# Filler matmuls taken out of a pipelined kernel, its first keys computed earlier, and three softmax sums moved from GpSimd to TensorE

## The reference

```
xn = layernorm(x)
# layer 0: causal attention, 16 heads of 8, keys and values from a 32-wide latent; beside it 8 experts, top 2 of them
lat = layernorm(xn @ W_dkv); k = rope(lat @ W_uk); v = lat @ W_uv; q = rope(xn @ W_q)
x = x + (softmax(causal(q k^T)) v) @ W_o + sum_e gate_e * (relu(xn @ W1[e] + b1[e]) @ W2[e] + b2[e])
xn = layernorm(x)
# layer 1: attention of 16 heads, mixed with two attentions of 4 heads of 32; beside it a gated three-layer FFN
ctx = softmax(mod * q k^T) v
ctx = 0.3 * ctx + 0.7 * mha4(xn)          # "ca"
ctx = 0.85 * ctx + 0.15 * mha4(ctx)       # "mc"
x = x + ctx @ W_o + ffn(xn)
```

## Time and profile before

| what | value |
|---|---|
| runs, median (lowest to highest) | 1742.61 us (1740.61 to 1746.71) |
| the profiled execution: time, span | 1751.61 us, 1749.9 us |
| mean granted TensorE clock in it | 0.949 of 2.4 GHz |
| busy share PE, DVE, ACT, POOL | 88%, 69%, 60%, 47% |
| POOL's sums for the denominators (L1423) | 64 instructions, 149.2 us busy |

### The profile page before, as it was taken

One profiled execution on the slowest core, in us unless ns is written; L12 is line 12 of the kernel. 1 busy time (PEld: TensorE's weight loads), 2 busy tenths in 40 slices (PEclk: granted clock), 3 DMA queues, 4 the chain that ended last, 5 costly groups with the idle time before them and its releaser, 6 DMA issues.

```text
span 1749.9 us, 33947 instructions
## 1 busy us (share of the span) xinstructions
PE 1539.8 (88%) x11449; PEld 655.0 (37%) x11449; DVE 1202.1 (69%) x3135; ACT 1055.2 (60%) x2322; POOL 817.4 (47%) x728
## 2 busy tenths in 40 slices
PE   2587799889999999999999999999899999889877
PEld 1353353235333543345333543345333533232222
DVE  6553578667885789667975788678976677477523
ACT  2273375667657766676656765677557765736542
POOL 4246355435644555454645455354654461513142
PEclk9998698999999999999999999999999999979877
DMA  5851471136211541236212631145203620201010
GB/s 210 259 152 50 128 195 33 46 93 181 79 42 61 154 118 55 67 93 180 63 34 75 166 103 48 63 117 157 69 29 96 185 80 7 61 13 37 0 37 6
DMA packets 138876, 159.35 MB, mean 91 GB/s; under 512 B 15744, under 2 KB 100304, under 8 KB 137808
## 3 DMA queue, kind: packets, MB, share of 16 engines
q1 hardware_dynamic: 134608, 148.79, 29.1%
q0 software_dynamic: 4096, 8.40, 1.6%
HBM read 115.96 MB, written 40.85 MB: 90 GB/s over the span
## 4 chain that ended last, share of the span: by engine, by line
PE 61%; DVE 11%; ACT 10%; issue 8%; POOL 6%; DMA 3%; SPq 2%; POOLq 0%; ACTq 0%; DVEq 0%
PE banks L450 58%; DVE negmax L862 6%; ACT probs L1202 3%; ACT hm L1271 3%; POOL psums L1423 2%; DMA qkc<-relm 1%; ACT L1202 1%; DVE h L1086 1%; PE banks L714 1%; POOL halves L1379 1%; PE banks L667 1%; SPq L1554 1%; POOL w L1442 1%; ACT h L1320 1%; DVE h L1081 0%
## 5 line engine op out<-in xcount | busy, mean ns | idle before, releaser
L1202 ACT ACTIVATE probs<-banks 128x512 f32<-128x512 f32 (+3 forms) x1216 | 582.5, 534 | 362.1 <-PE banks L450 340.2
L862 DVE TENSOR_REDUCE negmax<-banks 128x1 f16<-128x512 f32 x768 | 491.9, 685 | 157.5 <-PE banks L450 153.9
L858 DVE CUSTOM_DVE_ANT_0 scr<-banks,mask_row 128x384 bf16<-128x384 f32 (+3 forms) x512 | 230.2, 487 | 156.0 <-PE banks L450 146.0
L450 PE MATMUL banks<-kp,qs 32*128 32x512 f16 (+3 forms) x1024 | 239.6, 360 | 64.4 <-DMA kp<-relk 21.1
L450 PE MATMUL banks<-probs,vp 128*32 128x512 f32 (+3 forms) x2048 | 241.1, 544 | 0.2 <-POOL probs L1375 0.2
L450 PE MATMUL banks<-qs,kp 32*128 32x512 f16 (+3 forms) x1024 | 218.3, 352 | 23.3 <-ACT probs L1202 15.9
L1463 POOL TENSOR_TENSOR h_lo<-h,h_hi 128x512 f16<-128x512 f32 x96 | 114.5, 1211 | 211.8 <-ACT h_hi L1314 116.0
L1403 POOL TENSOR_TENSOR hl<-hm,hh 128x512 f16<-128x512 f32 x120 | 139.9, 1168 | 136.3 <-DVE hh L1028 136.3
L1423 POOL TENSOR_TENSOR psums<-psums,probs 128x1024 f32<-128x1024 f32 x64 | 149.2, 2356 | 113.1 <-PE banks L450 113.1
L1271 ACT ACTIVATE hm<-banks,wt 128x128 f32<-128x128 f32 x480 | 137.7, 374 | 72.2 <-PE banks L450 71.7
L450 PE MATMUL banks<-qkc 97*128 97x512 f16 (+1 forms) x512 | 169.6, 404 | 8.8 <-DVE negmax L862 3.0
(11 more groups left out here) (211 smaller groups left out, 2457.1 us busy)
## 6 DMA issues: line engine op xcount, KB each, us to landing
wt<-wexp SPq DMA_DIRECT2D x120, 258.0 KB, 3.0
wt<-wexp SPq DMA_DIRECT2D x120, 256.0 KB, 3.0
qkc<-relm SPq DMA_DIRECT2D x96, 128.0 KB, 3.2
qs<-relq SPq DMA_DIRECT2D x64, 128.0 KB, 2.5
kp<-relk SPq DMA_DIRECT2D x64, 128.0 KB, 2.6
relm<-halves SPq DMA_DIRECT2D x32, 256.0 KB, 2.1
xg<-xslots SPq DMA_DIRECT2D x24, 256.0 KB, 3.0
yslots<-yv SPq DMA_DIRECT2D x24, 256.0 KB, 3.5
```

The lines of the kernel that those rows point to most:

```text
L450: return nc.tensor.matmul(psum[rows_, bank, cols_], lhsT, rhs, start=start, stop=stop)
L858: v.tensor_tensor_reduce(scr[:, s, 0:kw], psum[:, SCO + s, 0:kw], mask_row[:, T - kw:T], -1.0, 3e38, ALU.add, ALU.min, negmax[:, g.n % 2, ...
L862: v.tensor_reduce(negmax[:, g.n % 2, NC * h + c:NC * h + c + 1], psum[:, SCO + s, 0:kw], AX.X, ALU.max, negate=True).then_inc(sem("max"), 1)
L1202: a.activation(keys(g, c)[:, 2 * pair + s, q0:T], psum[:, TRA + s, q0:T], ACT.Exp, scale=SCALE[main(g)]).then_inc(sem("exp"), 1)
```

## The change

Three edits. The fillers of `turn_over` go, in every period. The first batch's keys get a stage of their own, 8 steps earlier, which puts them ahead of `pos`, `gates` and `starts` of its routing, and the first two stores of the weights move from G = -11 and -10 to -4 and -3, behind the first two `spread`s; one lot of `keep_warm` of the first batch moves from G = 52 to 47. For the last three 4-head groups (`direct`) PE sums every block of keys itself, POOL's sums go, and POOL multiplies quarter by quarter.

```
-TURNS = (6, 3, 3)
-MOVE = {"route": {0: 6}, "warm0": {-1: -6}, "warm1": {-1: 6}, "front": {}, "prep": {0: 11},
+MOVE = {"route": {0: 6}, "warm0": {-1: -6}, "warm1": {-1: 6}, "front": {}, "keys": {0: -8}, "prep": {0: 11},
-AT.update({("w_store", i): at for i, at in enumerate((-11, -10, -4, 2), 0)})
-AT.update({("turn", i): at for i, at in enumerate((72, 6, 47), 0)})
+AT.update({("w_store", i): at for i, at in enumerate((-4, -3, -2, 2), 0)})
...
+    elif head.split("_")[0] in ("k0", "k0r"):
+        STAGE[name_] = "keys"
...
+        def direct(g):
+            return g.mix >= len(MIXES) - 3
...  value(), PE
-                    last.then_inc(sem("pv"), 1)
-                    if not main(g) and c == NC - 1:
+                    if direct(g):
+                        if c == 0:
+                            own("n", "den", g.n)
+                        if c == NC - 1:
+                            last.then_inc(sem("pv"), 1)
+                        for h in range(GH):
+                            last = mm(N, slice(0, T), ones[:, :], keys(g, c)[:, h, :], c == 0, c == NC - 1,
+                                      rows_=slice(32 * h, 32 * h + 32))
+                        last.then_inc(sem("n_full" if c == NC - 1 else "pv"), 1)
+                    else:
+                        last.then_inc(sem("pv"), 1)
+                    if not main(g) and not direct(g) and c == NC - 1:
...  the loop of PE
-                    turn_over(G)
...  mixing(), DVE
                                 if k == NC - 1:
                                     ins.then_inc(sem("n_taken"), 1)
+                                elif direct(g):
+                                    ins.then_inc(sem("quarter"), 1)
...  exp_unit(), ACT: no wait for psums
+                                if not direct(before):
+                                    act.wait_ge(sem("psums"), 4 * before.mix + 2 * k - 1 + pair)
...  mixing(), POOL
+                            pool.wait_ge(sem("out_taken"), g.n + 1)
+                            if direct(g):
+                                for k in range(NC - 1):
+                                    pool.wait_ge(sem("quarter"), (NC - 1) * (g.mix + 3 - len(MIXES)) + k + 1)
+                                    p_.tensor_tensor(out=oc[:, ch(k)], in0=oc[:, ch(k)], in1=r_b[:, ch(k)], op=ALU.mult)
+                            left = slice(P * (NC - 1), T) if direct(g) else slice(0, T)
                             taken(pool, "n", "den", g.n)
-                            pool.wait_ge(sem("out_taken"), g.n + 1)
-                            p_.tensor_tensor(out=oc[:, :], in0=oc[:, :], in1=r_b[:, :], op=ALU.mult).then_inc(sem("oc"), 1)
+                            p_.tensor_tensor(out=oc[:, left], in0=oc[:, left], in1=r_b[:, left], op=ALU.mult).then_inc(sem("oc"), 1)
...  the loop of POOL
-                        if not main(g) and 2 <= j < 6:
+                        if not main(g) and not direct(g) and 2 <= j < 6:
```

More of the change, by code:

```diff
@@ L146 @@
 AT.update({("y_store", i): at for i, at in enumerate((20, 29, 37, 43), 0)})
-AT.update({("w_store", i): at for i, at in enumerate((-11, -10, -4, 2), 0)})
-AT.update({("turn", i): at for i, at in enumerate((72, 6, 47), 0)})
-AT.update({("warm0", i): at for i, at in enumerate((34, 37, 43, 47, 48, 51, 58, 65, 66, 70), 0)})
+AT.update({("w_store", i): at for i, at in enumerate((-4, -3, -2, 2), 0)})
+AT.update({("warm0", i): at for i, at in enumerate((34, 37, 43, 47, 48, 51, 53, 65, 66, 70), 0)})
 AT.update({("warm1", i): at for i, at in enumerate((178, 181, 186, 188, 192, 192, 194, 194, 197, 199), 0)})
@@ L594, in opening @@
                             project(N, W(w), xT[:, :]).then_inc(sem("n_full"), 1)
[L596 to L603, removed]
                 def keep_warm(G):
@@ L1196, in exp_unit @@
                             if k in (1, 2):
-                                act.wait_ge(sem("psums"), 4 * before.mix + 2 * k - 1 + pair)
+                                if not direct(before):
+                                    act.wait_ge(sem("psums"), 4 * before.mix + 2 * k - 1 + pair)
                             elif pair == 0:
```

## The result

| | median (lowest to highest) | profiled execution: time, span, mean clock |
|---|---|---|
| before | 1744.11 us (1740.61 to 1746.71, 4 runs) | 1751.61, 1749.9 us, 0.949 |
| after | 1762.34 us (1761.01 to 1765.82, 4 runs) | 1763.57, 1761.4 us, 0.932 |

The ratio is 1.0097, 95% interval [1.0071, 1.0123]: slower by 18 us, where 1745 was forecast and the range ended at 1758.

The account below looks back on a forecast made before the run. The prediction took PE as the bound, with 61% of the chain that ended last. From 1742.6 us it took 9 (start), 0.9 (warm lot) and 1.2 (tail) and added 13.4 (falls): 1744.9, forecast 1745, range 1729 to 1758.

Parts of the forecast that it names:

- Direct gain 0: At the fillers' three places: removing 87 matmuls gains 0 us, since PE still waits for ACT or DVE; bounds 0 to 37.
- first three: First lot of three fillers per period: eight gaps of 2.1 us, 0.5 of them falling at 0.9 us each, 3.6 us lost.
- The falls' cost, 13.4 us: Where fillers stood: 22 longer PE gaps bring falls of the granted clock to 1.2 GHz, 13.4 us lost; bounds 0 to 35.
- the start: First batch: earlier keys and later stores bring the first weight load from 67.22 to about 58, gain 9 us; bounds 4 to 12.
- warm lot: First batch: four matmuls moved ahead of its last sums leave the chain there, gain 0.9 us; bounds 0 to 1.7.
- the tail: Last three 4-head groups: PE's own sums gain 1.2 us net; bounds 3.5 gain to 2.5 loss.
- six: Lot of six fillers per period: seven gaps of 2.3 us, 0.8 of them falling at 1.5 us each, 8.4 us lost.
- second three: Second lot of three fillers per period: seven gaps of 1.7 us, 0.4 of them falling at 0.5 us each, 1.4 us lost.
- the last group's 1.8: Last 4-head group: 1 us from no wait for POOL's sums and 0.8 from POOL's smaller last product, gain 1.8 us.
- the group of `ca` of batch 7: Third direct group, which waits for no sum: eight more matmuls on PE cost 1.8 us where PE bounds, 1.5 taken.
- The rival of the many falls: Falls at nearly every bare place at full price, 16 at 1.57 us, 25 us lost: 1757 us; chance 0.2.
- The clock's rival: Without fillers the clock holds, or nearly, with about 2 more falls (3 us): 1734 us; chance 0.28.

Follow-up runs that it names:

- e5: The changed kernel with all fillers back and PE's direct sums only for the last two 4-head groups, early keys kept: 1735.68 us, ratio 0.9934 to before.
- e2: The kernel before with only the 87 fillers and their waits taken out: 1768.04 us, ratio 1.0126 to before.
- e12: The changed kernel as it is, run again on another chip: 1762.8 us, ratio 1.0111 to before.
- e1: The changed kernel with the fillers put back where they were, the keys' and direct sums' edits kept: 1741.61 us, ratio 0.9971 to before.
- e9: e5 with the three lots of fillers taken out: 1758.52 us, ratio 1.0074 to before.
- e3: The kernel before with only the early keys, the two later stores and the earlier warm lot, fillers kept: 1740.49 us, ratio 0.997 to before.
- e4: The kernel before with only the direct sums by PE in the last three 4-head groups, fillers kept: 1747.93 us, ratio 1.0007 to before.
- e6: The changed kernel with the lots of six fillers back, both lots of three still out: 1751.26 us, ratio 1.0027 to before.
- e11: e5 with a fourth lot of three fillers at G = 58 of each period: 1738.29 us, ratio 0.9973 to before.
- e10: e5 with fillers of 128 columns instead of 512, same number, places and waits: 1742.49 us, ratio 0.9994 to before.
- e8: The changed kernel with the fillers back in doubled lots (12, 6, 6): 1750.82 us, ratio 1.0021 to before.
- e7: The changed kernel with the fillers' waits back but not one matmul: 1757.14 us, ratio 1.0051 to before.

## Why the prediction was wrong, point by point

**Direct gain 0: right.** Stretches that keep their clock take the same time with and without fillers: 38.68 us in after and in e5. (From G = 16 to 40 the four kernels without fillers are 2.5 us shorter in all, on average, the only trace of a gain.) The gaps were read a little too high in number: of the eight places of the first three, five have the gap of 2.2 us; at G = 86 and 166 PE has shorter ones.

**The falls' cost, 13.4 us: this is the step that failed.** Measured 22 us (e2) and 24 us (e12 over e1, e9 over e5). The mechanism and its sign were as put; the number and places were not. The result is 16 us slower than the forecast (18.2 over before, where 2.3 was the sum): 9 of them are this term, 5 the start with its warm lot, 2 the tail. To split it, I took the stretches of a period apart and compared the mean of four kernels without fillers (after, e2, e9, e12) with that of five with them (before, e1, e3, e4, e5), summed over the middle:

| stretch | lot in it | us at 1.2 GHz, with / without | forecast us | measured us |
|---|---|---|---|---|
| G = 72 to 80 | six | 3.4 to 6.8 / 20.5 to 27.3 | 8.4 | 3.2 |
| G = 0 to 16 | first three | 26.8 to 31.7 / 55.7 to 57.7 | 3.6 | 8.1 |
| G = 40 to 56 | second three | 17.1 to 30.7 / 23.9 to 44.4 | 1.4 | 5.2 |
| the others | none | 6.8 to 15.6 / 6.8 to 13.7 | 0 | -1.6 |
| all of the middle | | 58.8 to 77.7 / 115.7 to 134.4 | 13.4 | 14.9 |

The places of the falls are what ties them to the lots. At G = 72 and 73 all 24 stretches of the four kernels without fillers have one, and none of the 30 with; at the first three, from G = 240 on, it is 19 of 20 against 0 of 25. (Of the us at 1.2 GHz in the second row, 23 to 34 are of the first of its seven stretches, in every kernel.)

In the middle alone the sum of 13.4 is nearly met, but by luck: three errors cancel. At the six the number was right (a fall at each), the price was not: the six stretches of after take 22.47 to 23.08 us, 0.5 to 1.1 more than a whole one of 21.97, and not 1.5. I put this down to ACT's exponentials, which hold PE for part of it; no run shows this by itself. With the lots, seven of the thirty stretches fall later, at G = 75 behind the wait for `w`, and take 23.55, so that 3.2 us are left. At the first three I took half of the lots at 0.9 us; it was five of six in after and all in e9 and e12 (one of the six, at G = 166, falls with fillers too), at 1.2 (39.96 and 39.85 against 38.68). At the second three, 0.4 of the lots at 0.5 us; there a fall costs 1.5 (39.8 against 38.3), and falls came at G = 40 to 45 too, where no lot had stood.

The rest came outside these 550 steps. In the pairs that differ in the fillers alone, e1 and e12, e5 and e9, the spans differ by 19.5 and 23.7 us, of which the middle has 15.6 and 18.7, what lies behind step 632 has 4.9 and 5.3, and the start -0.9 and -0.3. Most of the tail's loss, 3.5 us, comes between the first maxima of steps 688 and 692, where no lot stood. There e9 and e12 stand at 1.2 GHz for 13.7 us, e1 and e5 for 3.4. But e6, which has the only lot behind step 632, stands so for 13.7 us too, and so do before and e11 with all their fillers, while e2 without them has 6.8 us (262.2 and 258.4 us behind step 632). So the forecast had nothing for the tail, two pairs out of three show a loss there, and its cause stays open. And the medians stand above what profiled executions show, which for e2 and e12 were the lowest of their runs; a term that varies from execution to execution can't be sized from one execution.

**The start, -9: right in its steps, too large in its worth.** Step 80 came 9.0 us earlier in the two traces compared; in the three traces with the old start it stands at 182.0 to 185.0 us, in the eleven with the new one at 175.1 to 178.6, which is 7 us on average, and the timed gain of e3 is 5 (1 to 9). **The warm lot** wasn't separated from it. **The tail, -1.2:** the last group's 1.8 is 1.2 (from the first maximum of step 732 to the end 44.6 us in after and e12, 45.8 in before and e3), the group of `ca` of batch 7 cost 2.5 instead of 1.5; all three, e4, +0.07%.

**The rival of the many falls** (16 at 1.57 us, 25 us, 1757) comes nearest to what came, though not by its sum: the traces show 13 more falls on average, at 1.1 us each in the middle. It was given 0.2. What argued against it, that ACT and DVE hold PE behind 15 of the 22 gaps, was true for the six's place, where it was not applied, and false for the first three, where it was. With its 25 us, the start's 5 instead of 9, no gain from the warm lot and the tail, and 1744 for before it gives 1764. The range ended at 1758, below that: this rival was its slow case, and it had every other term at its likeliest value.

**The clock's rival** (1734) did not come. One argument for it was misread: the two windows of rows 3 have the same busy time, 8.51 and 8.50 us, but 48 and 56 matmuls, so the one that fell had done less work. The Trainium skill (TensorE: Matmul & The Clock Gate, "HAM oscillation — how this bites in real kernels") puts the drops down to idle gaps longer than any here; this trace disagrees, with a fall behind nearly every gap of 2.2 to 2.3 us (the one at 1154.20 above is the exception). Its next section, "A second HAM failure mode: psum-queue depth-cycling", tells of a kernel whose clock swung because of frequent short pauses; e10's stretch with pauses of 0.60 and 1.17 us agrees with that one.

## What to carry to other kernels

Matmuls that nobody reads can be worth keeping where they stand wholly behind a wait: 87 of them cost nothing and were worth 22 to 24 us of 1745; by the waits alone, which divide one of the gaps, some 10 us of this were kept. Before taking them out, look at the windows just behind each and count how many periods keep clock 1.00 with them; a lot protects its own stretch alone, and doubled it runs out of cover. Price a fall by the stretch that it would land in (0.5 to 1.1 us at the six's place, 1.2 to 1.6 at the others), once for every period, and measure the tail apart.

## What was not expected

- With all fillers kept the clock fell seldom but not never: 7 to 15 falls in the middle (4 in e11), most at G = 40 to 45 and 55 to 60 behind PE waits of 1.06 and 0.68 us or none. No kernel had none.
- A granted clock of 1.00 in the first 70 us may stand for no record at all. The same window of e12, then of e1:

```profile
39.00:61.00 22.00, 8.03 (x32) 3.62 (x31) 11.51 (x33) 3.61 (x6) 7.49 (x7) 0.50 0.78 248
```

```profile
39.00:61.00 22.00, 9.08 (x35) 3.96 (x35) 11.36 (x33) 3.61 (x6) 7.83 (x7) 1.00 0.79 253
```

But the matmuls take as long in both. The eight transposes of `xg` in e12, in e1 and in e8, whose records have 2.4 GHz just there:

```profile
52.41 1.04 PE L671 MATMUL banks<-ident,xg 128*128 128x128 f16 x8 [4.40 <-DMA xg<-xslots]
```

```profile
52.83 1.03 PE L682 MATMUL banks<-ident,xg 128*128 128x128 f16 x8 [3.69 <-DMA xg<-xslots]
```

```profile
52.60 0.62 PE L682 MATMUL banks<-ident,xg 128*128 128x128 f16 x8 [2.39 <-DMA xg<-xslots]
```

So e1 was at 1.2 GHz there as well. The clock's records begin at 19 us in e6, e8, e10 and e12, and at 71 to 84 us in the other ten, and what lies ahead of them counts as full. The mean clock of e12, 0.918, would be 0.934 without its records of the first 78 us, as after's 0.932 is. Mean clocks compare only between traces whose records begin at the same place.
- A quarter of the filler columns behind the same waits (e10) had already 0.80% of the 1.40%, and the waits with no matmul at all (e7) 0.60%.
